# Scores of depth-8 heads from three bf16 parts of q and k, in place of fp32 products, in a chain of four attention layers

## What is computed

```python
x = L0(x, ctx, mask)    # softmax(q k^T/sqrt(8) * m - (1-m)*1e10) v, wo, + x, LayerNorm
x = L1(x, ctx)          # RMS norm, 16 heads of depth 64, + x
x = L2(x, ctx)          # self attention: causal, blocks of 64 kept or dropped by a router;
                        # cross attention ("LC" in the kernel); feed-forward 512; each + x
x = L3(x, ctx)          # softmax((q+bq)(k+bk)^T/sqrt(8)) v, wo, + x, LayerNorm
```

## Time and profile before

| | us |
|---|---|
| median of 3 runs (lowest, highest) | 382.58 (382.28, 383.41) |
| the profiled execution | 382.29 |
| its span | 380.6 |
| PE busy | 336.4 (88%) |
| DVE, ACT, POOL busy | 241.7, 200.9, 90.8 |

### The profile page before, as it was taken

One profiled execution on the slowest core, in us unless ns is written; L12 is line 12 of the kernel. 1 busy time (PEld: TensorE's weight loads), 2 busy tenths in 40 slices (PEclk: granted clock), 3 DMA queues, 4 the chain that ended last, 5 costly groups with the idle time before them and its releaser, 6 DMA issues.

```text
span 380.6 us, 9089 instructions
## 1 busy us (share of the span) xinstructions
PE 336.4 (88%) x3621; PEld 212.6 (56%) x3621; DVE 241.7 (64%) x458; ACT 200.9 (53%) x419; POOL 90.8 (24%) x254
## 2 busy tenths in 40 slices
PE   4779998997989989998898999979999998999981
PEld 1334445665778778867543444445455665565550
DVE  6524366527986666859647778788565446546834
ACT  1345656647686668676523435344555534445550
POOL 7114242300300001003045113413413304313311
PEclk9999999999999999999999999999999999999997
DMA  7266000000000000000000000001000000000000
GB/s 229 95 232 255 0 3 3 2 2 0 2 0 3 2 2 0 2 2 28 29 0 22 36 29 28 16 3 43 22 30 10 2 14 16 2 16 9 22 15 29
DMA packets 7450, 11.94 MB, mean 31 GB/s; under 512 B 2024, under 2 KB 4464, under 8 KB 7152
## 3 DMA queue, kind: packets, MB, share of 16 engines
q1 hardware_dynamic: 6720, 10.04, 7.6%
q10 hardware_dynamic: 688, 1.32, 0.9%
HBM read 6.63 MB, written 0.52 MB: 19 GB/s over the span
## 4 chain that ended last, share of the span: by engine, by line
PE 67%; ACT 14%; DVE 10%; issue 5%; DMA 2%; POOL 1%; POOLq 0%; ACTq 0%; SPq 0%
PE psum L275 16%; PE psum L330 7%; PE psum L655 4%; PE psum L304 4%; PE psum L284 4%; PE psum L680 4%; PE psum L714 4%; ACT probs L381 3%; PE psum L566 3%; ACT probs L756 3%; PE psum L706 3%; ACT probs L764 3%; PE psum L631 3%; PE psum L691 2%; PE psum L874 2%
## 5 line engine op out<-in xcount | busy, mean ns | idle before, releaser
L452 DVE TENSOR_REDUCE maxs<-psum 128x8 f32<-128x1024 f32 x64 | 78.1, 1222 | 67.4 <-PE psum L265 28.1
L275 PE MATMUL psum<-km,qT 32*128 32x512 f32 x256 | 71.0, 634 | 17.6 <-ACT v1all L636 3.8
L381 ACT ACTIVATE probs<-psum 128x1024 f32<-128x1024 f32 x48 | 49.2, 1025 | 51.2 <-PE psum L304 49.8
L284 PE MATMUL psum<-qm,kT 32*128 32x512 f32 x256 | 72.1, 638 | 0.7 <-ACT probs L381 0.7
L275 PEld LDWEIGHTS psum<-km,qT 32*128 32x128 f32 x256 | 20.0, 183 | 31.7 <-issue 26.7
L330 PE MATMUL psum<-probs,vpad 128*32 128x128 f32 x1024 | 34.5, 275 | 2.1 <-DVE probs L462 2.1
L756 ACT ACTIVATE probs<-psum,maxs 128x128 f32<-128x128 f32 x128 | 34.9, 392 | 0.5 <-DVE maxs L804 0.5
L524 POOL TENSOR_SCALAR rstd<-stats 128x2 f32<-128x2 f32 (+1 forms) x18 | 6.7, 372 | 116.1 <-DVE stats L488 116.1
L330 PEld LDWEIGHTS psum<-probs,vpad 128*32 128x32 f32 x1024 | 26.2, 109 | 13.2 <-DVE probs L462 5.1
L431 POOL CAST mp<-maxs 128x16 bf16<-128x16 f32 x32 | 6.8, 214 | 98.3 <-DVE maxs L452 98.2
L304 PEld LDWEIGHTS psum<-mrow,sel 32*128 32x128 bf16 x512 | 17.4, 93 | 19.8 <-issue 18.2
(11 more groups left out here) (151 smaller groups left out, 622.6 us busy)
## 6 DMA issues: line engine op xcount, KB each, us to landing
km<-kT SPq DMA_DIRECT2D x30, 64.0 KB, 1.9
wmat<-in_wmat SPq DMA_DIRECT2D x1, 1856.0 KB, 13.2
qm<-qT SPq DMA_DIRECT2D x16, 64.0 KB, 1.9
wmat<-in_wmat SPq DMA_DIRECT2D x1, 1024.0 KB, 8.9
qm<-qT SPq DMA_DIRECT2D x32, 32.0 KB, 1.8
wrow<-in_wrow SPq DMA_DIRECT2D x1, 704.0 KB, 5.4
ctxT<-in_ctxt SPq DMA_DIRECT2D x2, 256.0 KB, 4.8
xnT<-in_xt ACTq DMA_DIRECT2D x2, 256.0 KB, 6.5
```

The source lines that it names most:

```text
L275: s_mm = e.matmul(bank(j), qT[rg(j), bt(b)], km[L.slot][rg(j), :, bt(b)], start=True, stop=L in (LC, L3), skip_group_check=True)
L284: e.matmul(bank(4 + a), kT[rg(j), M.slot, bt(b)], qm[rg(j), :, bt(b)], start=True, stop=False, skip_group_check=True)
L381: e.activation(probs_of(n, half), bank(4, 2), ACT.Exp, bias=masked, scale=layer(n).scale)\
L452: e.tensor_reduce(maxs[:, n % 2, 8 * half:8 * half + 8], bank(2 * half, 2).rearrange("p (h k) -> p h k", k=P), AX.X, ALU.max, negate=True)\
```

## The change

**Scores.** q and k are each cut into three bf16 parts. Six products (0·0, 0·1, 0·2, 1·0, 1·1, 2·0) lie as six slots of eight rows in a stack of 64 rows, `qs` and `ks`; a head is one 64-row, 128-column bf16 matmul, so S of a half is 8 of them with 8 weight loads, and T the same. A seventh slot holds L0's mask in `ks` (ones in `qs`), so `S_more` and the exp's bias go.

**Making the parts.** ACT writes part 0 (`act_p0`), DVE the rest (`dve_rest`), ACT part 1 (`act_p1`), GpSimd or DVE part 2 (`any_p2`). `stack_dma` sends each part to its slots: six DMAs for a group of batches where there were four; groups are of two or four batches. Projections are two matmuls of 64 output rows where there were four of 32.

**L2.** The router's factor goes to q alone. TensorE adds the causal mask to T of half 1, and DVE clamps half 0 alone.

**Order.** Two steps without a new item (`HOLES` = 2). In L0 two of L1's value products and the projections of batches 4 to 7 move ahead of item 0, and fewer lie in the odd halves. The second half of L2's batches is projected in two pairs, the first inside L1. LC's transposes and q projections move half a step earlier.

```diff
+HOLES = 2
+SLOTS = {"q": (0, 0, 0, 1, 1, 2), "k": (0, 1, 2, 0, 1, 0)}
...
-                for j in (2 * half, 2 * half + 1):
-                    s_mm = e.matmul(bank(j), qT[rg(j), bt(b)], km[L.slot][rg(j), :, bt(b)], start=True,
-                                    stop=L in (LC, L3), skip_group_check=True)
+                for c, r, rows, i in heads(half):
+                    s_mm = e.matmul(bank(2 * half + r)[:, bt(c)], qs[rows, i, bt(b)], ks[L.slot][rows, i, bt(b)],
+                                    start=(c == 0), stop=L is not L2, skip_group_check=True)
...
+                for c, r, rows, i in heads(mhalf):
+                    e.matmul(bank(4 + r)[:, bt(c)], ks[M.slot][rows, i, bt(b)], qs[rows, i, bt(b)],
+                             start=(c == 0), stop=False, skip_group_check=True)
...
+            if m is not None and M is L2 and mhalf:
+                for a in range(2):
+                    e.matmul(bank(4 + a), causal[:, 0, :], identB[:, :].unsqueeze(1).broadcast_to([P, 4, P]),
+                             start=False, stop=False, skip_group_check=True)
...
+        def heads(half):
+
+            return [(c, r, slice(HD * r, HD * r + HD), 2 * c + half) for c in range(4) for r in range(2)]
...
+            for n, part in enumerate(SLOTS[name]):
+                if part == p:
+                    e.dma_start(to[n::8, :, toks(b0, nb)], parts[name][:, p, toks(b0, nb)])\
+                     .then_inc(sem(f"{name}s{b0}"), 16)
...
-            send_rows(e, L0, "k", 0, 4, (0, 1))
...
+            stack_dma(e, L0, "k", 0, 2, 0)
+            stack_dma(e, L0, "k", 0, 2, 1)
+            e.wait_ge(sem("kaug_out"), 1)
+            for k in range(3):
+                e.dma_start(ks0[8 * k + ROW_SLOT::HD, :, :], kaug[G // 2 * k:G // 2 * k + G // 2, :])\
+                 .then_inc(sem("kaug_in"), 16)
+            stack_dma(e, L0, "k", 0, 2, 2)
+            stack_up(e, L0, "k", 2, 2)
+            stack_up(e, L0, "q", 2, 2)
+            stack_up(e, L0, "k", 4, 4)
+            stack_up(e, L0, "q", 4, 4)
             e.dma_start(wcol[:, :], wcol_d).then_inc(sem("in_cols"), 16)
             e.dma_start(x[:, :, :], x_d).then_inc(sem("in_x"), 16)
             e.dma_start(wrow[:, :], wrow_d.partition_broadcast(P)).then_inc(sem("in_rows"), 16)
...
+            act_p0(e, L0, "k", 0, 4)
+            act_p0(e, L0, "q", 0, 4, 1)
+            e.wait_ge(sem("qs_one"), 1)
+            stack_dma(e, L0, "q", 0, 2, 0)
+            act_p1(e, L0, "k", 0, 2)
+            act_p1(e, L0, "q", 0, 2)
+            stack_dma(e, L0, "q", 0, 2, 1)
             e.wait_ge(sem("kaug_mm"), 1)
             e.copy(kaug[:, :], bank(3).bitcast(BF16)).then_inc(sem("kaug_out"), 1)
+            stack_dma(e, L0, "q", 0, 2, 2)
...
+                if s == 1:
+                    act_p1(e, L0, "k", 4, 4)
+                    act_p1(e, L0, "q", 4, 4)
...
             def even0(s):
+                if s == 2:
+                    any_p2(e, L0, "k", 4, 4)
+                    any_p2(e, L0, "q", 4, 4)
```

More of the change, by code:

```diff
@@ L252, in T_ready @@
         def T_ready(e, n, half):
-            if half == 0:
-                for what, count in data_of_T(n):
-                    e.wait_ge(what, count)
             if n == 0 and half == 0:
-                e.wait_ge(*L0.past("v_out", 1))
-                e.wait_ge(*L0.past("k_out", 2))
+                e.wait_ge(*L0.v_done("v_out", 0))
+                e.wait_ge(sem("k_raw"), 2)
             if 2 * n + half:
                 e.wait_ge(sem("exp_done"), 2 * n + half)
[L262 to L267, removed]
+        def heads(half):
+            return [(c, r, slice(HD * r, HD * r + HD), 2 * c + half) for c in range(4) for r in range(2)]
         def pe_scores(e, n, half, m, mhalf, turned=None):
@@ L377, in act_exp @@
                 e.wait_ge(sem("V_mm"), n - 1)
[L378 to L381, removed]
+            e.activation(probs_of(n, half), bank(4, 2), ACT.Exp, scale=layer(n).scale)\
              .then_inc(sem("exp_done"), 1)
@@ L445, in pool_attn @@
                     pool_split(e, n)
+                behind(s)
         def dve_max(e, n, half):
@@ L488, in dve_stats, with dve_attn @@
             e.bn_aggr(stats[:, b, :], stats6[:, b, :]).then_inc(sem(f"stats_{n}"), 1)
-        def dve_attn(e, steps, lo, hi, even, odd):
+        def dve_attn(e, steps, lo, hi, even, odd, end_of_even=lambda s: None):
             for s in steps:
@@ new lines, in act_p0 @@
+        def act_p0(e, L, name, b0, nb, to=None, c0=0):
+            out = parts[name][:, 0, toks(b0, nb)]
+            e.wait_ge(*L.mm_done(f"{name}_mm", b0))
+            bias = (L.bq if name == "q" else L.bk) if L.bq is not None else 0.0
+            if L.at:
+                for b in range(b0, b0 + nb):
+                    for what, count in LAYERS[L.at - 1].stacked(name, b):
+                        e.wait_ge(what, count)
+            if L is L0 and name == "k":
+                e.wait_ge(sem("k_raw"), b0 // 4 + 1)
+                src = rest_of(name, b0, nb)
+            else:
+                src = bank(to)[:, c0:c0 + nb * P]
+            if L is L2 and name == "q":
+                e.wait_ge(sem("keep"), 1)
+                for c in range(2):
+                    done = e.activation(blocks(out, c), blocks(src, c), ACT.Identity, scale=keep[:, c:c + 1])
+            else:
+                done = e.activation(out, src, ACT.Identity, bias=bias,
+                                    scale=E ** -0.5 if L is L0 and name == "q" else 1.0)
+            done.then_inc(sem(f"{name}_p0"), 1)
@@ L570, in pe_v, with stack_up @@
+        def stack_up(e, L, name, b0, nb):
+            for p in range(3):
+                stack_dma(e, L, name, b0, nb, p)
         def pe_v(e, L, g, to):
```

601 lines of the change are left out of this document (352 added, 249 removed).

## The result

The changed kernel takes 408.4 us, median of 4 runs (406.8 to 412.3), against 382.8 (382.3 to 383.4) for the kernel before in the same comparison: a ratio of 1.069, 95% interval 1.064 to 1.073. It is slower by 25.6 us, where 22 less were forecast. The profiled execution has a span of 405.0 (380.6 before). Medians and ranges here are over all executions of a kernel; the ratios leave out those over 1.5% above its fastest.

A forecast was written before the change was run, and what follows sets the result against it. It took TensorE, busy 88% of the span, as the main bound, with DVE near its limit in L2. From 382.29: 13.7 - 9.0 - 1.7 + 0 - 10 - 4 - 11 = -22.0, so 360.3 us; range 346 to 377.

The forecast's parts named there:

- Score group: S and T of a half: sixteen bf16 matmuls in 0.55 to 0.6 us, against 1.07 or 1.6 before.
- the 0.054 a matmul: Score matmuls by the skill's load rule, two groups side by side: at best 0.054 us each, time about 383.
- Start: Up to step 3: late `wrow` holds GpSimd and TensorE's transpose of item 2, plus 1.1 for low clock: +13.7 us.
- Rest of L0: Five steps after the start: less value-product, score and mask work, 7.6 to 5.75 us a step, -9.0.
- L1 and its edges: L1 at 0 (-2 to +4), and halves that fill and drain behind L0 at -1.7: together -1.7 us.
- L2, LC, L3: Shorter steps from less TensorE work: L2 -10 us at 6.2 a step, LC -4, feed-forward, L3 and tail -11.
- the last stretch: Step 22 to the end, feed-forward, L3 and tail: -11 us of 93.1, including +3 for one more step.
- the light ones: Steps without extras in the last stretch: 5.3 us becomes 4.15.
- The clock: TensorE's lower clock after its stall of some 10 us at the start: 1.1 us added (0 to 3).
- Second empty step: One more step without a new item before L3, but with two light ones: +3 us.
- The causal half on T: L2: TensorE pays 0.53 us an item for the mask on T, DVE loses one clamp of 1.25.
- The rivals: Late weights don't hold, 350 (0.12); DMA issues cost double, 376 (0.12); loads bind, 375 (0.10); matmuls slow, 399 (0.07).

The follow-up runs named there:

- experiment 1: Changed kernel with SP issuing wcol, x and wrow ahead of L0's two last stacks instead of behind them: 397.4 us.
- experiment 5: experiment 1 plus 73 extra bf16 matmuls where TensorE waited, ahead of the first S and of seven waits in L3: 388.0 us.
- experiment 6: experiment 5 plus an own rest buffer for each half of k and L1's T2 rows made one place earlier: 383.4 us.
- Experiment 4: Changed kernel with most of the parts' computing left out in L2, LC and L3: 393.1 us without transfers of parts 1 and 2, 394.3 with them.
- experiment 7: Kernel before the change with two empty steps ahead of L3's items instead of one: 387.5 us.
- experiment 9: experiment 6 plus a changed SP stack order (380.4 us), with VectorE again clamping both halves in L2 and no causal term on T: 389.6 us.
- the best version: experiment 6 plus changed SP stack order, LC's transposed copies ahead of the exp, and 36 more extra matmuls in L2 and LC: 377.5 us.
- the last two: On experiment 6 with changed SP stack order: LC's transposed copies ahead of the exp, 379.0 us; then 36 more extra matmuls, 377.5 us.
- experiment 3: Changed kernel with an own piece of the rest buffer for each half of k: 408.6 us (400.4 to 411.8).

## Why the prediction was wrong

- **Score group: right.** 0.56 for sixteen. The Trainium skill (TensorE: Matmul & The Clock Gate, LDWEIGHTS) gives a load its columns over 1.2, 107 ns for 128. The recorded loads are near that, 98 ns on average, but the 0.054 a matmul that the prediction made of it, with two loads at a time, does not hold for this form: eight with their own loads start every 0.028 us.
- **Start: mechanism right, size short.** +17.2 for +13.7. `wrow` was issued 5.0 us later than worked out. Of these, 2.7 are there at item 0's S: ScalarE's table load of 1.28 stands ahead of its part 0, behind the wait for VectorE (in the kernel before it ran at 3.28, ahead of a wait, and delayed nothing), and the forecast had it at nothing; the other 1.4 were not taken apart. The remaining 2.3 come from item 0's S to the issue, while TensorE's clock was low from 20 to 28: a value product's four records take 3.52 there and 1.98 behind. I had counted the low clock only behind the stall. Of the 17.2, experiment 1 (the order) takes away 7.8 and experiment 5 (the clock) 3.3; the other 6.2 stay, since item 0's S comes 8.8 later than before (20.78 and 12.02).
- **Rest of L0: near at full clock, in part by luck.** Once nothing stalls it takes 29.3 (experiments 1, 5, 6), -8.6 for a forecast -9.0, 5.86 a step for 5.75. But the terms listed for a step (0.86, twice 0.5, 0.25) add up to 2.1 and would have given 5.5; the 5.75 has no working. In the changed kernel 4.0 went to the low level.
- **L1 and its edges: +3.6 for -1.7.** The changed kernel turns L2's rows in item 4 instead of item 5 of L1. TensorE waits 2.27 there for VectorE's `xn`, which stands behind a division that waits for ScalarE, and later 1.14 for a rest of q. This was in the diff, and I charged it at nothing.
- **L2, LC, L3: the step that failed.** I set a step's length equal to TensorE's sum of work, with no idle time at all, though L2 had 4.0 of it before. The sums were right: in experiment 6 it is busy 37.72 / 6 = 6.3 a step in L2 (6.2 forecast) and 5.7 / 6 = 0.95 less than before in LC (-1). But idle time, 4.0 of 47.1 before, became 8.6, and in LC 4.0 became 10.3. What came off TensorE was a wait for VectorE, ScalarE, GpSimd or SP in the same step. Experiment 4 says which: of L2's and LC's missing 9 and 5 us, the parts with their transfers are 2.5 and 4.8 (43.8 and 36.0 against experiment 6): all of LC's, and a quarter of L2's, whose other 7 were there without them, 6.2 of them as idle time, mostly behind copies that the next S waits for. In the last stretch, by experiment 6, L3's seven steps from item 24 on are 6.3 shorter than before (0.9 each, where the light ones were to give 1.15) and the tail 1.3, but the stretch with the two empty steps is 5.9 longer and the steps ahead of it 1.2: 0.4 is left of the 11.
- **The clock: not in the sum beyond the start.** I had a row of it at the end and used it for one stall. It fell in five more stretches (16 to 28, 244 to 252, 260 to 268, 296 to 304, 336 to 360). Experiment 5 prices the like of the first and the last at 3.3 and 6.0. The Trainium skill (TensorE: Matmul & The Clock Gate, HAM oscillation) tells of a kernel whose TensorE waits for data again and again and loses its clock each time. This trace agrees for the waits of 6.6 and 9.9; it also fell behind one of 2.6, and did not behind one of 2.27 in L1. The fall should have been a rival with a price.
- **Second empty step: +4.8 for +3** (experiment 7).
- **The causal half on T: right in sign** for the whole kernel, and larger than I had it (9.2 in experiment 9). By what way is open: L2, where the gain was forecast, moved by 1.1.
- **The rivals** turned on the price of a matmul, of a transfer or of the start. None was of the kind that came: TensorE's work falls as planned and the time does not.

From the changed kernel to the best version, 30.9 us come back in six places: 11.0 from the order of three loads, 9.4 from extra matmuls, 4.6 from a buffer and a place in L1, 3.1 from SP's order, 1.3 and 1.6 from the last two. What remains between 377.5 and the forecast of 360.3 is, by the stretches of that kernel, L2 45.4 for 37, LC 40.2 for 36, the end 90.0 for 82, and L1 with its edges 131.4 for 127.6: 24 us, by the waits mostly idle time in chains through all engines, which no run here removed. Against them stands the start, 38.9 for 46.7, since the stall that was forecast is gone.

## What to carry to other kernels

When an engine that bounds a kernel gets less to do, the forecast needs the idle time of the new step, not only the new sum: go through each step's waits and ask which ones its work had covered. Where a change makes TensorE wait for 1 to 3 us in a row of places, price the lower clock behind them, and see whether cheap matmuls into a free place hold it up. And put loads whose readers stand in another engine's queue ahead of transfers that depend on late work.

## What the runs showed of the hardware

- TensorE's clock fell behind a single wait of 2.6 (244 to 252 in the changed kernel) and behind pairs of 1.5 and 1.8 with work between, but not behind one of 2.27 in L1. Which stretches fell changed with edits elsewhere: low stretches in L1 at 152 to 160 or 164 to 172 came and went with the code of L1 unchanged. The executions scatter with it: 11 us in experiment 3 (mean clock 0.944 in the fastest, 0.911 in the slowest), where the kernel before had 0.5 beside it.
- Adding 73 small matmuls (384 bf16 columns each) made the kernel 9.4 us faster.
- ScalarE's table load takes 1.28 us and stands right ahead of its first activation. Where that one waited for other work (8.96 in the changed kernel) the load came behind the wait and was paid in full; in the kernel before it came at 3.28, with 3.49 of waiting behind it.
- Eight bf16 matmuls of 64 x 128, each with an own load of 94 to 98 ns, start 0.22 us apart as a group (0.028 each) when they alternate between two row groups of 64; with the change to 32-row groups behind it a group takes 0.34, and the eight 32-row ones 0.33.
- Transfers of 64 KB within the core land 2.0 us after issue and their issues cost SP 0.60 each; half of them left out in L2 to L3 moved the median by 1.2 us, within the scatter.
